# Score and maximum products of the attention phases issued as strips of 32 output rows

## What is computed

```python
scores = jnp.einsum('bhqd,bhkd->bhqk', q, k) / jnp.sqrt(jnp.float32(dh))
attn = jax.nn.softmax(scores, axis=-1)
out = jnp.einsum('bhqk,bhkd->bqhd', attn, v).reshape(B, Lq, H)
return x_q + (out @ Wp + bp)
```

## Time and profile before

| | |
|---|---|
| median of 3 executions | 6477.11 us (6474.23 to 6477.28) |
| the profiled execution | 6475.3 us, span of the trace 6473.5 us |
| PE busy | 5939.3 us, 92% of the span, 49714 matmuls |
| PE weight loads | 3112.4 us, 48% |
| ACT busy | 4237.2 us, 65% |
| DVE busy | 4119.5 us, 64% |
| POOL busy | 981.5 us, 15% |
| granted PE clock | 0.98 of full on average |

### The profile page before, as it was taken

One profiled execution on the slowest core, in us unless ns is written; L12 is line 12 of the kernel. 1 busy time (PEld: TensorE's weight loads), 2 busy tenths in 40 slices (PEclk: granted clock), 3 DMA queues, 4 the chain that ended last, 5 costly groups with the idle time before them and its releaser, 6 DMA issues.

```text
span 6473.5 us, 147216 instructions
## 1 busy us (share of the span) xinstructions
PE 5939.3 (92%) x49714; PEld 3112.4 (48%) x49714; DVE 4119.5 (64%) x6523; ACT 4237.2 (65%) x8158; POOL 981.5 (15%) x1660
## 2 busy tenths in 40 slices
PE   6999999999877899999999977789999999999998
PEld 3444444444444444544454444444444444445665
DVE  5767677677555667766776445467777777754443
ACT  3777777777666577777777556557777777773333
POOL 3121121121111111111111011212212212200000
PEclk9999999999999899999999989899999999999999
DMA  2322322222111322232232011122232232220110
GB/s 88 78 65 56 79 59 63 75 56 69 42 57 61 82 68 65 69 79 69 57 76 75 1 57 57 55 77 68 57 77 68 57 77 68 57 65 21 54 53 29
DMA packets 180915, 402.05 MB, mean 62 GB/s; under 512 B 16992, under 2 KB 124560, under 8 KB 166416
## 3 DMA queue, kind: packets, MB, share of 16 engines
q1 hardware_dynamic: 180752, 400.01, 22.9%
HBM read 316.81 MB, written 83.14 MB: 62 GB/s over the span
## 4 chain that ended last, share of the span: by engine, by line
PE 73%; issue 8%; ACT 8%; DVE 7%; DMA 2%; SPq 1%; POOL 1%; ACTq 0%; DVEq 0%; POOLq 0%
PE bank L1140 19%; PE bank L1186 18%; PE pair L1156 14%; DVE MX L1480 3%; PE bank L1112 2%; ACT P L1316 2%; PE bank L1107 2%; DMA QP<-scr_q 2%; PE pair L1173 2%; PE pair L1162 1%; PE bank L699 1%; PE bank L690 1%; ACT QP L1327 1%; PE pair L626 1%; DVE ST L1437 1%
## 5 line engine op out<-in xcount | busy, mean ns | idle before, releaser
L1316 ACT ACTIVATE P<-bank 128x512 f32<-128x512 f32 (+1 forms) x5504 | 3102.2, 597 | 1350.6 <-PE bank L1140 1306.9
L1480 DVE TENSOR_REDUCE MX<-pair 128x2 f32<-128x802 f32 x3072 | 2923.9, 988 | 1296.3 <-PE pair L1156 1288.0
L1140 PE MATMUL bank<-QP,KP 128*128 128x256 bf16 (+1 forms) x11008 | 2091.3, 277 | 141.7 <-ACT P L1316 90.0
L1186 PE MATMUL bank<-P,VA 128*25 128x256 f32 (+1 forms) x22016 | 1756.0, 391 | 5.8 <-issue 0.5
L1156 PE MATMUL pair<-KP,QP 96*128 96x401 bf16 x6144 | 1576.0, 338 | 60.9 <-DMA QP<-scr_q 42.3
L1140 PEld LDWEIGHTS bank<-QP,KP 128*128 128x128 bf16 (+1 forms) x11008 | 858.0, 100 | 1577.3 <-ACT P L1316 912.9
L1186 PEld LDWEIGHTS bank<-P,VA 128*25 128x25 f32 (+1 forms) x22016 | 401.7, 102 | 711.0 <-issue 456.7
L1156 PEld LDWEIGHTS pair<-KP,QP 96*128 96x128 bf16 x6144 | 593.5, 98 | 181.7 <-DVE MX L1480 64.0
L1605 POOL COPY VA<-VN 128x416 f32<-128x416 f32 (+1 forms) x320 | 138.6, 434 | 2520.6 <-PE bank L1186 2439.1
L1484 DVE TENSOR_REDUCE MX<-pair 128x4 f32<-128x1024 f32 x256 | 311.3, 1223 | 326.8 <-PE pair L1162 326.2
L1327 ACT CAST QP<-pair 2x512 bf16<-2x512 f32 x640 | 338.9, 575 | 130.1 <-PE pair L1173 124.7
(11 more groups left out here) (246 smaller groups left out, 4497.5 us busy)
## 6 DMA issues: line engine op xcount, KB each, us to landing
KP<-scr_k SPq DMA_DIRECT2D x192, 900.6 KB
QP<-scr_q SPq DMA_DIRECT2D x960, 48.0 KB
CN<-ctx_n SPq DMA_DIRECT2D x40, 768.0 KB
scr_k<-KSF SPq DMA_DIRECT2D x48, 600.8 KB, 3.3
scr_k<-KSF SPq DMA_DIRECT2D x48, 600.0 KB, 3.3
CT<-ctx_t SPq DMA_DIRECT2D x24, 800.5 KB, 4.4
KP<-scr_ks SPq DMA_DIRECT2D x128, 144.0 KB
scr_q<-QS SPq DMA_DIRECT2D x80, 192.0 KB, 2.1
```

The source lines that it names most:

```text
L1140: last = nc.tensor.matmul(SC[half][0:kt, k * N:(k + 1) * N], KP[g][:, c0:c0 + kt], QP[g][:, h * N:(h + 1) * N], start=True, stop=True)
L1186: last = nc.tensor.matmul(OB[32 * h:32 * h + STEP + HD + 1, 0:N], VA[g % 2][0:kt, t, h, :], P[(g * ph.nt + t) % 2][0:kt, h * N:(h + 1) * N ...
L1316: nc.scalar.activation(P[v % 2][0:kt, half * 2 * N:(half + 1) * 2 * N], SC[half][0:kt, :], ACT.Exp, scale=SCALE).then_inc(sem("probs_full" ...
L1480: nc.vector.tensor_reduce(MX[:, r, c:c + 2], MP[j % 2][:, :].rearrange("p (t k) -> p t k", t=2)[:, :, 0:SPANS[0][1]], AX.X, ALU.max).then_ ...
```

## The change

Every product in `scores` and `maximum` is issued as up to four, each for 32 columns of the stationary operand and so for 32 output rows. The data, the results and the order are as before; the moving operand is read by each of the four. The last tile of a cross phase (65 keys) becomes 32, 32 and 1. Only the last strip of the last product signals the semaphore.

```diff
+            def strips_of(out, lhsT, rhs, start=True, stop=True):
+
+                n = lhsT.shape[1]
+                for c in range(0, n, 32):
+                    m = min(32, n - c)
+                    last = nc.tensor.matmul(out[c:c + m, :], lhsT[:, c:c + m], rhs, start=start, stop=stop)
+                return last
...
-                    last = nc.tensor.matmul(SC[half][0:kt, k * N:(k + 1) * N], KP[g][:, c0:c0 + kt],
-                                            QP[g][:, h * N:(h + 1) * N], start=True, stop=True)
+                    last = strips_of(SC[half][0:kt, k * N:(k + 1) * N], KP[g][:, c0:c0 + kt],
+                                     QP[g][:, h * N:(h + 1) * N])
...
-                        last = nc.tensor.matmul(MP[j % 2][:, k * 512:k * 512 + n],
-                                                QP[g][0:MR, h * N + qt * 128:h * N + qt * 128 + 128],
-                                                KP[g][0:MR, h * ph.nk + c0:h * ph.nk + c0 + n], start=True, stop=True)
+                        last = strips_of(MP[j % 2][:, k * 512:k * 512 + n],
+                                         QP[g][0:MR, h * N + qt * 128:h * N + qt * 128 + 128],
+                                         KP[g][0:MR, h * ph.nk + c0:h * ph.nk + c0 + n])
...
-                            last = nc.tensor.matmul(MP[j % 2][:, (2 * k + qt) * N:(2 * k + qt + 1) * N],
-                                                    QP[g][0:MR, h * N + qt * 128:h * N + qt * 128 + 128],
-                                                    KP[g][0:MR, h * ph.nk:(h + 1) * ph.nk], start=True, stop=True)
+                            last = strips_of(MP[j % 2][:, (2 * k + qt) * N:(2 * k + qt + 1) * N],
+                                             QP[g][0:MR, h * N + qt * 128:h * N + qt * 128 + 128],
+                                             KP[g][0:MR, h * ph.nk:(h + 1) * ph.nk])
```

## The result

The changed kernel takes **6679.6 us** (median of four runs, 6633.4 to 6688.2) against 6477.2 before: 1.030 times the time before, 95% interval 1.025 to 1.035. The forecast was 6381, so it is slower where I forecast faster, and outside the range. The profiled execution took 6688.2 us.

What follows compares the result with a forecast made beforehand. PE was taken to bound the kernel. Savings of 1.5 us per `a0` and `c2` element and 3.4 per `c1`, with +0.2 per self element, made -48, -54 and +6, together -96 on 6475.3: forecast 6381 us, range 6290 to 6600.

Steps and rivals of the forecast that it cites:

- What bounds it: Whole kernel: PE holds 73% of the chain, and a cross element is as long as PE's own program.
- what a change of width costs: Between 128-row and quarter-width products: 0.09 us in, 0.10 back; removing changes saves 0.24 a tile, 12.5 a cross element.
- Strips at no cost: Scores and maxima: four quarter-width products run side by side in one product's time, surcharge taken as zero.
- rival 1: Scores, maxima and `head_values`: each set of four costs 0.02 us more, giving 6590 to 6600 us; chance 0.16.
- 3: Scores and maxima: bf16 strips do not run side by side, some 13,000 us; chance 0.04.
- the sequencer keeps up: PE's sequencer: at most 0.025 us per load and matmul pair, 1.0 us for a 1.55 us tile; nothing counted.
- rival 4: PE's sequencer does not keep up: 0.06 us a pair, 111 us for 1851 pairs, some 7200 us; chance 0.03.
- Pieces pay 0.30: 128-row pieces among strips pay 0.30 us each: 5.4 us an element in `a0` and `c2`, 4.2 in `c1`.
- Given back at ScalarE and VectorE: Cross elements: waits return 2.9 us at ACT, 2.0 at DVE, and 0.7 for statistics in `a0` and `c2`.
- rival 2: PE's cross loops: the body may no longer stay on the core; jumps cost 0 to 88 us, 6381 to 6470; chance 0.13.

Runs made afterwards that it cites:

- run 9: Kernel before, with strips of 32 rows in only three tiles of each cross element (2035 records in the body); 6472.3 us, ratio 0.999.
- run 10: Changed kernel with TensorE's middle-element loops written out (no jump) and the loop loads of packed keys cut to 64 columns; 6395.2 us.
- run 6: Changed kernel with strips of 64 rows instead of 32 (2599 records in a body); 6909.1 us, ratio 1.067 to the kernel before.
- run 17: Strips only in chosen cross tiles without pieces, first three groups, and TensorE's loop branch hint removed; 6531.2 us, against 6400.6 with the hint.
- run 1: Changed kernel with TensorE's middle-element loops written out, so no jump; 6527.8 us, ratio 1.008 to the kernel before.
- run 5: Kernel before, without strips, with TensorE's middle-element loops written out; 6502.1 us, ratio 1.004.
- runs 14 to 16: Strips only in cross tiles without pieces, rest as before: in the loop 6464.4 us, written out 6357.6, in the loop with first three groups only 6400.6.
- run 14: Strips only in cross tiles without pieces (26 in `a0` and `c2`, 28 in `c1`), loops kept; 6464.4 us, ratio 0.998 to the kernel before.
- run 3: Kernel before with 52 spare semaphore increments in each cross element, one per tile (1979 records); 6494.0 us, ratio 1.002.

## Why the prediction was wrong

- **What bounds it, and what a change of width costs: right.** 0.09 on the way in, 0.10 back, 0.24 a tile: run 9 has them one tile at a time, run 10 over the whole kernel.
- **Strips at no cost (rival 1, 3), the sequencer keeps up (rival 4): right.** The eight strips of two heads take 0.22 us.
- **Pieces pay 0.30: right**, by the tiles of run 6 (2.34 to 2.67 us, while tiles without a piece stay at 1.80 and 1.81), and of run 10: 2.26 to 2.32 and 2.23 to 2.30 us, where -0.24 and +0.30 make +0.06.
- **Given back at ScalarE and VectorE: right in sum.** Run 10 has 96.9 and 90.2 us an element. The split is not: PE's waits for `P` are 182.7 us in it against 90.0 before, 1.9 us a cross element where I had 2.9, and those for the maxima 36.6 against 16.2, 0.4 where I had 2.0. Something else costs the difference, so that the sum holds by luck in part.
- **The step that failed is rival 2, code loading**, in two sentences. "The loop carries a hint for its jump, so I take zero", bounded by "at most about a small transfer's 2.1 us": the taken branch lasts 3.1 to 3.4 us. That is 39 jumps with 110 us of idle PE, and the clock behind them. The hint was taken at its word, with no row that showed a jump to code not resident. And "the blocks of one pass are then loaded while others run, [...] which straight code does already" was read at 20 records a us; at twice that density a block that waits behind data stops PE in mid product.
- **What it cost.** The profiled executions of the changed kernel and of run 10 lie 293 us apart. PE's issue waits differ by 143 us (169.4 against 26.7), 110 of them at the jumps. Half clock differs by 197 us, at 0.41 each 81 (an estimate: the 0.41 is from the two rows of run 10). Waits for the `QP` loads differ by 23 (133.4 against 110.0). The other 46 us I can't assign. The clock was in no step of mine; I had no rival in which idle PE costs more than the idle time.

The Trainium skill ("Runtime: NRT & Kernel Launch", Instruction fetch mechanics) gives 2048 instructions for PE: 2035 records stayed, 2187 were fetched anew, so the runs agree. It says that a taken branch to an absent block stalls, and that crossing a block is mostly hidden; the first holds without a hint (3.5 us in run 17), the second doesn't hold here for dense code beside heavy loads (93 us of waits in run 1, 11 in run 5 with half the code). The Trainium skill ("TensorEngine Tiling (Array Packing)", Key Properties) has it that changing the tiling mode drains the engine. The traces agree: 0.09 to 0.10 us here, between 64 and 32 rows too.

**Still open:** why the half clock falls behind some gaps and not others (behind the jump at 2411 us, with a gap as long, it stays at 1.00, and run 10 has some with no gap), whether the last block decides the branch as the table has it (spare records at the end of a body would tell), and what holds back the gain of runs 14 to 16.

## What to carry to other kernels

Before an edit that multiplies instructions, count the records of each loop body of that engine, and how many it uses up in a us beside the heaviest loads. Where the body doesn't stay, a branch hint does not make the jump free by itself: measure the taken branch, and look where the body ends among its blocks of 256 records. An edit that changes the mode of an engine pays at every border, so convert whole stretches between two borders that exist anyway, and leave those alone that other work cuts through. If the sum is a small difference of large terms, look for the subset with the gain and without the price: written out, 26 to 28 of 52 tiles gave 1.9% and all of them lost 0.8%; in the loop, 18 to 20 gave 1.2%, 26 to 28 gave 0.2% and all lost 3.0%.

## What the runs showed of the hardware that I had not expected

- A taken branch to code that must be fetched lasts 3.5 to 4.7 us without a hint. With one it lasts 0.35 to 0.56 us where 87 or more records lie in the body's last block of 256, and 1.5 to 3.6 where at most 78 do, at 2599 records as at 3911, and equally dense ends can have either (run 14: 0.45 and 3.37 us).
- Leaving a loop has a price too: with bodies of some 2035 records (run 9) PE waits 4.5 to 6.0 us behind each cross loop, with 1979 (run 3) 4.9 behind two of them; with 1927 it doesn't.
- 260 increments of a semaphore that nobody waits for came with 4.4 to 6.0 us an element, 52 with none. That the sequencer has room for one in a tile and not for five is my reading; the body of 260 is also fetched anew.
- Code blocks wait behind data: with the DMA engines 75% busy, one came 15 us after the last instead of mostly 4 to 8, and with light loads PE's waits away from the jumps fell from 60 us to 16.
